# Low-rank mixes in pairs on four row tiles, a first direct pass in one matmul, and a new order of steps

## The reference

```python
xn = ln(x);  sx = token_shift(xn, previous)
xxx = tanh((xn + sx * maa_x) @ maa_w1)            # (l, 5, 32)
xxx = matmul(xxx, maa_w2)                         # five low-rank mixes, (l, 5, E)
x5  = xn[:, :, None] + sx[:, :, None] * (maa_stack + xxx)
w = exp(-exp(time_decay + tanh(x5[1] @ decay_w1) @ decay_w2))
r, k, v = x5[3] @ Wr.T, x5[0] @ Wk.T, x5[2] @ Wv.T;  g = silu(x5[4] @ Wg.T)
# per head: out_t = r_t . (u * k_t v_t + s);  s = w_t * s + k_t v_t     (a scan over tokens)
x = x + groupnorm(out) * g @ Wo.T
xn2 = ln(x);  sx2 = token_shift(xn2, previous)
x = x + sigmoid((xn2 + sx2 * b) @ ffn_Wr.T) * (square(relu((xn2 + sx2 * a) @ ffn_Wk.T)) @ ffn_Wv.T)
```

## Time and profile before

| | us |
|---|---|
| median of 3 runs | 807.27 (805.28 to 808.2) |
| the profiled execution | 808.39 |
| its span, first to last instruction | 806.6 |
| mean granted TensorE clock over it | 0.97 of full |

### The profile page before, as it was taken

How to read it: one execution, slowest core, us unless ns; L and a number is a source line. 1 busy time by engine, 2 the same in 40 slices (tenths; PEclk the granted TensorE clock), 3 DMA queues, 4 the chain that set the end, 5 groups by cost and what they waited for, 6 DMA issues and landing times.

```text
span 806.6 us, 18247 instructions
## 1 busy us (share of the span) xinstructions
PE 713.7 (88%) x7708; PEld 501.1 (62%) x7708; DVE 513.8 (64%) x766; ACT 323.3 (40%) x634; POOL 375.2 (47%) x224
## 2 busy tenths in 40 slices
PE   6876899997999979998899979997999978997797
PEld 5763676566674656656674656655765656745783
DVE  2848874696657775597557866586636963476540
ACT  2211654247341752327432572317433373325311
POOL 1028345573458435573357445483256634573001
PEclk9986899999999999999999999999899999999699
DMA  6910001010010101010010200101010000100000
GB/s 182 394 31 28 9 2 39 16 54 9 2 53 1 61 2 35 21 53 9 2 53 1 60 2 2 52 25 36 2 43 11 27 8 2 53 1 28 2 1 26
DMA packets 19421, 28.95 MB, mean 36 GB/s; under 512 B 5904, under 2 KB 11920, under 8 KB 18320
## 3 DMA queue, kind: packets, MB, share of 16 engines
q1 hardware_dynamic: 19344, 27.80, 10.8%
HBM read 18.35 MB, written 4.19 MB: 28 GB/s over the span
## 4 chain that ended last, share of the span: by engine, by line
PE 56%; DVE 16%; issue 11%; ACT 10%; POOL 5%; DMA 1%; SPq 0%; POOLq 0%; DVEq 0%; ACTq 0%
PE FB L545 14%; PE BAB L754 7%; PE FA L772 6%; PE FB L553 6%; PE FA L793 5%; PE BAB L671 3%; POOL pp L472 3%; ACT half L971 3%; DVE kvs L1238 2%; PE FA L806 2%; DVE half L1206 2%; PE FA L610 2%; ACT pp L958 2%; PE FB L585 2%; PE BAB L731 2%
## 5 line engine op out<-in xcount | busy, mean ns | idle before, releaser
L472 POOL TENSOR_TENSOR pp<-rT,kT 128x2048 f32<-128x2048 f32 (+1 forms) x32 | 108.6, 3403 | 44.9 <-DVE rT L1142 44.9
L439 POOL TENSOR_TENSOR mixes<-mixes 128x1024 f32<-128x1024 f32 x28 | 67.4, 2405 | 124.7 <-ACT mixes L895 124.7
L545 PE MATMUL FB<-mixes,wk_s 128*128 128x256 f32 x256 | 63.0, 401 | 6.9 <-POOL mixes L441 3.5
L441 POOL TENSOR_TENSOR mixes<-mixes,xnT 128x1024 f32<-128x1024 f32 x28 | 67.4, 2408 | 2.2
L1222 DVE TENSOR_REDUCE half<-half 128x256 f32<-128x2048 f32 (+2 forms) x32 | 64.5, 2014 | 0.5
L545 PE MATMUL FB<-mixes,wv_s 128*128 128x256 f32 x256 | 60.8, 381 | 3.1 <-POOL mixes L441 3.0
L488 POOL TENSOR_TENSOR acc<-acc,half 128x512 f32<-128x512 f32 x32 | 41.1, 1284 | 47.6 <-DVE half L1222 46.3
L545 PE MATMUL FB<-mixes,wg_s 128*128 128x256 f32 x256 | 62.2, 392 | 0.0
L772 PE MATMUL FA<-wide,fk_s 128*128 128x256 f32 x256 | 57.2, 381 | 3.7 <-DVE wide L1354 2.4
L545 PEld LDWEIGHTS FB<-mixes,wk_s 128*128 128x128 f32 x256 | 49.7, 199 | 16.6 <-issue 4.7
L545 PEld LDWEIGHTS FB<-mixes,wg_s 128*128 128x128 f32 x256 | 48.5, 195 | 18.3 <-issue 12.5
(11 more groups left out here) (136 smaller groups left out, 1342.9 us busy)
## 6 DMA issues: line engine op xcount, KB each, us to landing
pp<-x SPq DMA_DIRECT2D x8, 512.0 KB, 4.0
xt<-x SPq DMA_DIRECT2D x8, 512.0 KB, 3.7
vp<-vT SPq DMA_DIRECT2D x128, 32.0 KB, 1.9
out<-wide SPq DMA_DIRECT2D x8, 512.0 KB, 3.0
wk_s<-wk SPq DMA_DIRECT2D x1, 1024.0 KB, 4.9
wv_s<-wv SPq DMA_DIRECT2D x1, 1024.0 KB, 6.9
thR<-thB SPq DMA_DIRECT2D x16, 64.0 KB, 2.0
wr_s<-wr SPq DMA_DIRECT2D x1, 1024.0 KB, 7.2
```

What stands on the lines that cost most here:

```text
L439: nc.gpsimd.tensor_tensor(slot, slot, sx, ALU.mult).then_inc(s_["mixm_ready"], 1)
L441: nc.gpsimd.tensor_tensor(slot, slot, xnT[:, :, 1:L + 1], ALU.add).then_inc(s_["mix_ready"], 1)
L472: ins = nc.gpsimd.tensor_tensor(pp[:, i % 2, 0:size].rearrange("p (n i j) -> p n i j", i=m, j=m), spread(r.unsqueeze(3), 3, m), spread(k.u ...
L545: ins = nc.tensor.matmul(dst[:, c * L:(c + 1) * L], weight[:, q, c * P:(c + 1) * P], src[:, q, :], start=(q == 0), stop=(q == C - 1))
```

## The change

Mixes 1 and 2 are computed in one step, f_m21, and mixes 3 and 4 in f_m23; f_m22 and f_m24 are gone. Mixes 1 and 3 go to FA, 2 and 4 to BB, so that the four 32-row tiles write four banks. BB is shared, so waits are added: f_m21 waits until the chunk states of the same walk are copied (kvhalf_ready), f_m23 until b_gn's rows are (y1_ready), b_gn until mix 2 is evicted, b_norm2 until mix 4 is. GpSimd writes the two products of the first direct pass beside each other for each of the four column groups, and b_score0 takes them in one matmul of 384 columns. The first walk's warming matmuls go from 34 to 4. The order of steps is written anew on all engines; VectorE's main list alone is as before, as is its second.

```diff
 tensor, first:
-            warm6 f_norm warm2 warm8 warm4 f_lora0 f_lora1 f_m20 warm14 f_m21 f_dec1 f_dec2 f_m22 f_k0 f_k1 f_k2
-            f_m23 f_k3 f_v0 f_v1 f_v2 f_r0 f_v3 f_r1 f_r2 f_r3 f_m24""".split(),
+            f_norm warm4 f_lora0 f_lora1 f_m20 f_dec1 f_m21 f_dec2 f_k0 f_k1 f_m23 f_k2 f_k3 f_v0 f_v1 f_v2 f_v3
+            f_r0 f_r1 f_r2 f_r3""".split(),
 tensor, main:
-            c_fk b_score0 c_fr0 c_fr1 b_score1 c_fv0 b_score2 c_fv1 b_g0 b_score3 f_norm b_g1 b_score4 b_g2 b_g3
-            b_vtok f_lora0 f_lora1 b_ktok f_m20 b_kv0 b_kv1 f_m21 f_dec1 f_m22 f_dec2 b_acc f_k0 f_k1 b_apply0
-            b_apply1 b_apply2 b_apply3 f_k2 f_k3 f_v0 f_m23 b_gn0 f_v1 b_gn1 f_v2 b_wo0 f_m24 b_wo1 f_v3 f_r0
-            f_r1 b_norm20 f_r2 b_norm21 f_r3""".split(),
+            c_fk b_score0 c_fr0 b_score1 c_fv0 b_g0 b_score2 c_fr1 c_fv1 b_score3 f_norm b_g1 b_score4 b_g2 b_g3
+            b_vtok f_lora0 f_lora1 b_ktok f_m20 b_kv0 b_kv1 f_dec1 f_m21 f_dec2 b_acc f_k0 f_k1 b_apply0
+            b_apply1 b_apply2 b_apply3 f_k2 f_k3 f_v0 f_v1 b_gn0 b_gn1 f_v2 f_m23 b_wo0 f_r0 b_wo1 f_v3 f_r1
+            b_norm20 f_r2 b_norm21 f_r3""".split(),
 vector, first:
-            f_xin f_mix0 n_stats f_mix1 f_mix2 f_centre n_norm f_mix3 f_mix4""".split(),
+            f_xin f_mix0 n_stats f_mix1 f_mix2 f_centre f_mix3 n_norm f_mix4""".split(),
 gpsimd, second:
-            b_prod0 b_prod1 b_prod2 b_prod3 b_prod4 b_add1 b_add2 f_sx b_add3 b_add4 b_s0 f_mix1 f_mix2 n_stats
+            b_prod0 b_prod1 b_prod2 b_prod3 f_sx b_prod4 b_add1 b_add2 b_add3 b_add4 b_s0 f_mix1 f_mix2 n_stats
 gpsimd, main:
-            b_prod0 b_prod1 b_prod2 b_add1 b_prod3 b_prod4 c_out0 b_add2 b_add3 c_out1 f_sx b_add4 b_s0 f_mix1
+            b_prod0 b_prod1 b_add1 b_prod2 b_prod3 b_prod4 b_add2 c_out0 c_out1 f_sx b_add3 b_add4 f_mix1 b_s0
             f_mix2 n_stats f_mix3 b_wo0 f_mix4 b_wo1""".split(),
 gpsimd, last:
-            b_prod0 b_prod1 b_prod2 b_prod3 b_s0 b_prod4 b_add1 b_add2 b_add3 c_out0 c_out1 b_add4 b_wo0 b_wo1""".split()),
+            b_prod0 b_prod1 b_prod2 b_prod3 b_prod4 c_out0 b_add1 c_out1 b_add2 b_add3 b_add4 b_s0 b_wo0 b_wo1""".split()),
 scalar, main:
-            c_fk0 c_fk1 c_fr0 c_fr1 b_rcopy f_norm b_g0 b_g1 b_vtok f_lora0 f_lora1 b_ktok b_kv0 f_mix1 f_dec1
-            b_kv1 b_decays f_dec2 b_exp f_mix2 f_k0 b_sq0 b_sq1 f_k1 f_v0 b_gn f_mix3 f_mix4 f_v1 b_norm2 f_r0
+            c_fk0 c_fk1 c_fr0 c_fr1 f_norm b_g0 b_rcopy b_g1 b_vtok f_lora0 b_ktok f_lora1 b_kv0 b_kv1 b_decays
+            f_mix1 f_dec1 f_dec2 b_exp f_mix2 f_k0 b_sq0 b_sq1 f_k1 b_gn f_mix3 f_v0 f_mix4 f_v1 b_norm2 f_r0
...
             def f_m2(j):
...
+                def run(b, par, n):
+                    pe.wait_ge(s_["mixe_ready"], NMIX * b + j)
+                    if j == 1:
+                        pe.wait_ge(s_["turned_ready"], 32 * (b + 1))
+                        if not first(b):
+                            pe.wait_ge(s_["kvhalf_ready"], T * b)
+                    elif not first(b):
+                        pe.wait_ge(s_["y1_ready"], C * b)
+                    for two in range(2):
+                        for mix, bank in ((j, FA), (j + 1, BB)):
+                            for half_of in range(2):
+                                c = 2 * half_of + two
+                                g = (mix - 1 + 2 * half_of) % NG
+                                rows = slice(32 * g, 32 * g + 32)
+                                ins = nc.tensor.matmul(bank[:, c * L:(c + 1) * L], w2_s[rows, c * P:c * P + P],
+                                                       (thB, thR)[half_of][rows, :], start=True, stop=True)
+                            if two == 1:
+                                ins.then_inc(s_["m2_ready"], 1)
...
 b_score:
+                    if i == 0 and first(b):
+                        pe.wait_ge(s_["mixe_ready"], NMIX)
...
-                    at = 0
-                    for m, _, to in DIRECT[i]:
-                        w = {0: L, 1: L // 2, 2: L, 4: 2 * L, 8: 2 * L}[m]
-                        for c in range(C):
-                            for g in range(NG):
-                                rows = slice(32 * g, 32 * g + 32)
-                                ins = nc.tensor.matmul(groups[32 * c:32 * c + 32, g, to:to + w], hm_s[rows, rows],
-                                                       pp[rows, i % 2, at:at + w], start=True, stop=True)
-                            at += w
+                    w = (FIRST, L, 2 * L, 2 * L, 2 * L)[i]
+                    for c in range(C):
+                        for g in range(NG):
+                            rows = slice(32 * g, 32 * g + 32)
+                            ins = nc.tensor.matmul(groups[32 * c:32 * c + 32, g, 0:w], hm_s[rows, rows],
+                                                   pp[rows, i % 2, c * w:c * w + w], start=True, stop=True)
 b_gn(t), tensor:
+                    if not last(b):
+                        pe.wait_ge(s_["mixe_ready"], NMIX * (b + 1) + 3)
 b_norm2(t), tensor:
+                    if not last(b):
+                        pe.wait_ge(s_["mixe_ready"], NMIX * (b + 2))
 f_mix(j), scalar and vector: FA is read as mixed_in(j)
+        def mixed_in(j):
+            return BB if j in (2, 4) else FA
```

More of the change, by code:

```diff
@@ L35 @@
 NG = P // 32
+FIRST = L + L // 2
 Q = L // NG
@@ L79 @@
         last="""
-            b_step1 b_step2 b_mul0 b_mul1 b_step4 b_red1 b_mul2 b_red2 b_mul3 b_red3 b_mul4 b_step8 c_mul0
-            b_red4 c_mul1 b_gate0 b_kv b_scan b_exp b_var0 b_var1 b_root b_nrm0 b_nrm1 b_gate1 b_gn b_wo0 b_wo1
+            b_step1 b_mul0 b_step2 b_mul1 b_red1 b_step4 b_mul2 b_red2 b_mul3 b_red3 b_mul4 b_step8 c_mul0
+            b_red4 c_mul1 b_kv b_scan b_exp b_gate0 b_gate1 b_var0 b_var1 b_root b_nrm0 b_nrm1 b_gn b_wo0 b_wo1
             b_xhat20 b_xhat21 b_norm2 b_xr""".split()),
@@ L91 @@
             f_mix2 n_stats f_mix3 b_wo0 f_mix4 b_wo1""".split(),
         last="""
-            b_prod0 b_prod1 b_prod2 b_prod3 b_s0 b_prod4 b_add1 b_add2 b_add3 c_out0 c_out1 b_add4 b_wo0 b_wo1""".split()),
+            b_prod0 b_prod1 b_prod2 b_prod3 b_prod4 c_out0 b_add1 c_out1 b_add2 b_add3 b_add4 b_s0 b_wo0 b_wo1""".split()),
     scalar=dict(
         first="""
-            f_norm f_lora0 f_lora1 f_dec1 f_dec2 f_k0 f_k1 f_mix1 f_v0 f_v1 f_mix2 f_r0 f_r1 f_mix3 f_mix4""".split(),
+            f_norm f_lora0 f_lora1 f_dec1 f_dec2 f_mix1 f_k0 f_mix2 f_mix3 f_k1 f_v0 f_v1 f_r0 f_mix4 f_r1""".split(),
@@ L97 @@
         second="""
-            f_norm b_g0 b_rcopy b_g1 b_vtok f_lora0 b_ktok f_lora1 b_kv0 b_kv1 b_decays f_mix1 f_dec1 b_exp
-            f_dec2 f_mix2 b_sq0 b_sq1 f_k0 f_k1 b_gn f_v0 f_mix3 f_mix4 f_v1 b_norm2 f_r0 f_r1""".split(),
+            f_norm b_rcopy b_g0 b_g1 b_vtok f_lora0 b_ktok f_lora1 b_decays b_kv0 b_kv1 f_mix1 f_dec1 b_exp
+            f_dec2 f_mix2 b_sq0 b_sq1 f_k0 b_gn f_mix3 f_v0 f_k1 f_mix4 f_v1 f_r0 b_norm2 f_r1""".split(),
         main="""
-            c_fk0 c_fk1 c_fr0 c_fr1 b_rcopy f_norm b_g0 b_g1 b_vtok f_lora0 f_lora1 b_ktok b_kv0 f_mix1 f_dec1
@@ L588, in f_lora, with f_m20 @@
                 return run
+            def f_m20(b, par, n):
+                loaded("w2", 16 * 12)
+                pe.wait_ge(s_["th_ready"], 2 * b + 1)
+                if not first(b):
+                    pe.wait_ge(s_["xnT_ready"], b + 1)
+                for c in range(C):
+                    for t in range(T):
+                        rows, to = slice(LORA * t, LORA * t + LORA), t * E + c * P
+                        ins = nc.tensor.matmul(FA[:, to:to + P], w2w_s[rows, c * P:c * P + P], thA[rows, :],
+                                               start=True, stop=True)
+                ins.then_inc(s_["m2_ready"], 1)
@@ L590, in f_m2 @@
             def f_m2(j):
                 def run(b, par, n):
[L592 to L599, removed]
-                        for c in range(C):
[L601 to L608, removed]
-                            rows = slice(32 * g, 32 * g + 32)
-                            ins = nc.tensor.matmul(FA[:, c * L:(c + 1) * L], w2_s[rows, c * P:c * P + P],
-                                                   (thB, thR)[half_of][rows, :], start=True, stop=True)
@@ L816, in _ @@
                               f"c_fr{t}": c_fr(t)})
-            steps.update({f"f_m2{j}": f_m2(j) for j in range(NMIX)})
+            steps.update(f_m20=f_m20, f_m21=f_m2(1), f_m23=f_m2(3))
             steps.update({f"b_apply{i}": b_apply(i) for i in range(C)})
```

33 lines of the change are left out of this document (16 added, 17 removed).

## The result

The changed kernel takes 827.8 us, median of four runs (822.5 to 829.2), against 806.9 us before: a ratio of 1.024 with an interval of 1.021 to 1.027. It is slower, 2 us from the 830 that were forecast.

What follows compares the result with a forecast made beforehand. TensorE, busy 88%, bounds the kernel, with about 8 us of waits a walk. A main walk: +4.6 - 0.6 - 0.4 = +3.6 us, six +21.6, the rest 0; 807.3 + 21.6 = 829, with part of rival B 830; range 816 to 846.

Steps and rivals of the forecast that it cites:

- The pair and the merged pass: TensorE: a pair takes 1.09 us like one mix, 2.2 us back; the first direct pass takes 0.93 against 1.28.
- the first third: Start of a main walk, new order: only small waits for scores go, 0.4 us won, between 0 and 0.6.
- the stretch from b_wo0 on: End of a main walk, to c_fk: 0.6 us taken back of the fourth mix's 1.09.
- The scan 4.5 us late: Middle of a main walk: b_s0 comes after all of f_mix1 on GpSimd, so b_scan starts at 380.25 against 375.79.
- Carried on at today's distances: From b_scan on, later steps keep their distances: b_apply ends 4.5 us later, b_wo0 starts 4.6 later, at 404.0.
- rival B: The granted clock falls in the middle of each walk; k2 and k3 slower, +10 to +18, about 843 us; chance 0.15.
- My upper bound: In the clock rival, k2 and k3 take 1.8 to 3.6 us more a walk, put at +10 to +18 in all.
- Nothing covers it: Middle of a main walk: the scan's +4.5 us comes through whole, since expansions, b_apply and b_gn hang on it in line.
- Rival A: The wait for b_s0 doesn't show; a walk takes 1.6 us less, six -9.6, about 798 us; chance 0.12.
- The first walks: Walks ahead of the six main ones: first +1.5 for lost warming, second -1 from the pairs.
- My +1.5 for the warming: First walk, 30 of 34 warming matmuls lost: -0.5 to +3.8 us, taken at +1.5.
- The end of the program: The last walk, behind the six main ones: -0.5 us, between -1.5 and +1.

Runs made afterwards that it cites:

- changed_kept_busy: The changed kernel with its warming matmuls back and, in each main walk, 6 more behind f_m21 and 9 behind f_dec2: 820.3 us, ratio 1.017.
- warm_restored: The changed kernel with the warming matmuls of the first walk put back: 824.6 us, ratio 1.021.
- s0_and_warm: The changed kernel with b_s0 before f_mix1 in GpSimd's main list and the warming matmuls back: 842.7 us, ratio 1.042.
- kept_busy: s0_and_warm with 6 warming matmuls behind f_m21 and 12 behind f_dec2 in each main walk: 818.3 us, ratio 1.013.
- apply_first: s0_and_warm with b_apply before f_k0 and f_k1 on TensorE and the squares before the copies of k on ScalarE: 829.8 us, ratio 1.028.
- one_pair: s0_and_warm with mixes 1 and 2 single again, without their added waits, ScalarE's order there as before; mixes 3 and 4 stay paired: 808.8 us, ratio 1.0006.
- scan_first: one_pair with all state copies before f_mix1, expansions before f_dec2's evictions, b_apply before f_k0 to f_k3, 12 warming matmuls before b_acc: 816.0 us, ratio 1.013.
- pairs_two_by_two: changed_kept_busy with the loops of a pair turned, mix outermost: 821.5 us, ratio 1.018.

## Why the prediction was right, and where it was wrong

The time and its sign were right, and so was the path as far as b_scan. The cause was named too narrowly. That the total came within 2 us is in part luck: the main walks lost 4.4 us less than forecast (17.2 against 21.6) and what comes ahead of them 3.0 more (3.5 against 0.5).

*The pair and the merged pass.* Right in size: 1.15 us for a pair, 0.93 for the pass. The Trainium skill, "TensorEngine Tiling (Array Packing)", Theoretical Speedup, gives up to 4x where one side is 32; a mix uses two row tiles and a pair four, and the trace agrees that both take the same time. Right too that little of it shortens a walk, and it was less than I had. In the walk shown the first third won 0.36 us (forecast 0.4) and the stretch from b_wo0 on 0.4 (forecast 0.6). Over all six walks these come to 0.04 and 0.07 us a walk.

*The scan 4.5 us late.* Measured 4.66 us: the copies, mix 1, GpSimd, b_s0 and b_scan came within 0.35 us of the times that I had worked out, counted from f_lora0.

*"Carried on at today's distances".* Here the first size failed. I took the 4.15 us of b_scan along, and 1.9 of them were a wait for GpSimd, which by then is done. The expansions so begin 2.8 us late, not 4.5, b_wo0 starts 2.83 us late, and the walk shown took 94.26 us, +2.07 where I had +3.6. I had quoted, in the same part, a GpSimd addition of 2.97 us beside a working VectorE, and did not ask what the VectorE operation beside it paid.

*The clock.* Six times 2.07 is 12.4 of the 17.2 us that the six walks lost. The other 4.8 us lie in the longer walks, up to 97.46 us, whose mean clock is 0.93 to 0.98. How much of this is the clock isn't shown. In changed_kept_busy, with the clock at 0.96 to 1.00, the six walks took 572.3 us against 574.1 in the changed kernel; 15.4 of the loss stay, and a walk at clock 1.00 still takes 94.96. By the medians the added matmuls bring 4.3 us (824.6 to 820.3), and the intervals overlap. (The trace of warm_restored, with 581.9 us for the six, is of its slowest execution.) So rival B, which I gave 0.15 as a thing of 10 to 18 us, is some 2 to 4 us here. With b_s0 first and the warming back it is larger than I said: 24 us between s0_and_warm and kept_busy. Its place was wrong as well: I had k2 and k3 slow, and it takes hold at f_k0 and f_k1 already. The rule of the Trainium skill that I set beside it ("TensorE: Matmul & The Clock Gate", HAM oscillation: the clock falls back where waits between bursts are long) agrees with the windows of the run with b_s0 first, 0.50 from 381 to 396 us. My upper bound had a slip besides: six times 3.6 us is 21.6, not 18.

*"Nothing covers it" and the cause.* This is the step that failed. I put the loss on b_s0 behind f_mix1. The swap back did not return it (836.5 us), and the swap in the kernel before cost 3 us. What costs is that mixes 1 and 2 are a pair: f_m21 waits for the state copies, and ScalarE must make them all first. Mix 1 goes to ScalarE 11.3 us behind f_lora0 instead of 8.1, and f_k0 waits for mix 1 and stands before b_apply. With mixes 1 and 2 taken apart, f_k0 is at 15.25 again and the loss is gone; that b_apply stood behind f_k0 and f_k1 is shown by apply_first. With mix 1 that late, both places of b_s0 lose: late, b_scan waits for it; first, the expansions and mix 1 hold each other up. I had written that k0 and k1 also wait for mix 1, and let it pass since the scan came later still. Rival A went wrong in the same way: I asked what ScalarE would be ready for, 379.4, and not when TensorE, with f_k0 and f_k1 first in its list, would come to b_apply. Not separated by a run of its own: the wait, ScalarE's order, f_dec1 before f_m21 and b_gn's wait for mix 2, which one_pair took back together. scan_first, where mix 1 is 2.7 us late at ScalarE without the wait, says that the order on ScalarE alone makes most of the delay; the pair forces that order. No run has the single mixes with b_s0 late.

*The first walks.* +3.5 us, where I had +0.5 for the first two. My +1.5 for the warming was probably too little, since about 2.4 us (by the estimate above) came of it, within the bound of +3.8. A gain of 1 us in the second walk did not show. The end of the program, behind the six walks: -0.2 for -0.5.

Open stays a stall of 1.5 to 2.1 us among TensorE's small matmuls in some walks, in the kernel before too (the walk from 509.89) and in several others. The profile shows nothing that it waits for. It differs from walk to walk and from run to run, so single walks say little under about 2 us. It may be where the 1 us per walk of one_pair went (its undisturbed walks are 91.4 and 92.1 us), which is not shown.

## What to carry to other kernels

When a wait is added to a step, follow every reader of its result through each engine's fixed order, and take the latest of these paths, not the first that costs; then ask what binds next before calling one edit the cause. Work taken from the busiest engine buys nothing if the freed time is spent waiting, and the waits can cost again through the clock. An operation's duration taken from a trace may hold a wait for its neighbour, so look at what ran beside it before moving it.

## What the runs showed of the hardware

- GpSimd tensor_tensors of 128x1024 and VectorE operations that read two tiles in SBUF took turns wherever they met in the stretches above, whichever came first. A VectorE scan of 128x1024 takes 2.29 us alone, and 4.15 when it starts while GpSimd's addition is running: it ends 2.15 us after that one, in each of six walks. Expansions and mix 1 that meet go one behind the other in the same way (ends at 386.19, 388.36, 390.07 and 392.06): 3.80 us become 5.78 to 7.5 on VectorE, 2.35 and 2.17 become up to 3.72 and 3.62 on GpSimd. The Trainium skill, "GPSIMD Engine Reference", Specifications, has the two engines share SBUF interfaces, with contention where the VectorE operation has two inputs in SBUF; the trace agrees.
- Matmuls to four row tiles start together even if the program lists all of one pair of tiles first (pairs_two_by_two: four records in 0.04 us, two of them from behind four other matmuls, two of which had not started).
- 108 matmuls without use, put into the waits, made a kernel 24 us faster (842.7 to 818.3); its walks went from a clock of 0.90 to 0.97 to one of 0.98 to 1.00. In the changed kernel 90 of them brought 4.3 us, with overlapping intervals.
